# Two attentions on one core: a root taken on VectorE instead of GpSimd, and GpSimd's pieces in another order

## What is computed

```
tgt2 = attention with 16 heads of batch 0 (x[0] asks, ctx[0] answers); x = x + tgt2 for all batches
X = layernorm(ctx) * w1 + b1;  F = layernorm(x) * w2 + b2
attended = softmax(F X^T / 16) X
h = gelu(attended fc1^T + b)                      # 4 features per token
cross = h fc2^T + b2                              # 256 features, but of rank 5
nc = layernorm(cross) * w3 + b3
selfatt = softmax(nc nc^T / 16) nc
out = F + gamma2 * (cross + gamma1 * selfatt)
```

## Time and profile before

| | before |
|---|---|
| median of 3 runs | 236.84 us (236.83 to 241.5) |
| profiled execution | 236.88 us, of which its span 234.8 us |
| TensorE products busy | 209.6 us (89%) |
| VectorE busy | 182.5 us (78%) |
| ScalarE busy | 153.8 us (66%) |
| GpSimd busy | 146.7 us (62%) |

### The profile page before, as it was taken

One profiled execution on the slowest core, in us unless ns is written; L12 is line 12 of the kernel. 1 busy time (PEld: TensorE's weight loads), 2 busy tenths in 40 slices (PEclk: granted clock), 3 DMA queues, 4 the chain that ended last, 5 costly groups with the idle time before them and its releaser, 6 DMA issues.

```text
span 234.8 us, 4965 instructions
## 1 busy us (share of the span) xinstructions
PE 209.6 (89%) x1730; PEld 151.6 (65%) x1730; DVE 182.5 (78%) x360; ACT 153.8 (66%) x295; POOL 146.7 (62%) x240
## 2 busy tenths in 40 slices
PE   8999979987779999999999989997998898899760
PEld 8776646776556978789787867794766444454230
DVE  6499977779979988878778999993333867988673
ACT  2177865544546877778777896789558786677520
POOL 6536551467499999987987793934953288322320
PEclk9999999999999999999999999999999999999855
DMA  6990000084540554426535200000000004444458
GB/s 227 384 332 4 1 1 3 0 223 138 178 179 3 179 179 138 149 78 180 179 108 158 94 3 0 6 0 1 3 0 0 3 15 167 179 181 180 183 212 324
DMA packets 14712, 26.81 MB, mean 114 GB/s; under 512 B 1760, under 2 KB 1760, under 8 KB 14688
## 3 DMA queue, kind: packets, MB, share of 16 engines
q1 hardware_dynamic: 14400, 25.98, 32.3%
q10 hardware_dynamic: 288, 0.52, 0.7%
HBM read 18.11 MB, written 8.39 MB: 113 GB/s over the span
## 4 chain that ended last, share of the span: by engine, by line
PE 53%; DVE 20%; ACT 10%; POOL 8%; issue 6%; DVEq 0%; ACTq 0%; POOLq 0%
PE psum L1085 15%; PE psum L1022 9%; PE psum L1093 5%; DVE xN L381 4%; DVE bn L361 4%; PE psum L970 3%; PE psum L1123 3%; DVE Fall L596 2%; DVE hmax L399 2%; PE psum L1105 2%; PE psum L1205 2%; DVE nmax L523 2%; ACT L862 2%; PE psum L1238 1%; ACT E L887 1%
## 5 line engine op out<-in xcount | busy, mean ns | idle before, releaser
L1085 PE MATMUL psum<-XT,Fall 128*128 128x256 f32 x256 | 61.0, 381 | 1.7 <-ACT Fall L857 1.7
L1085 PEld LDWEIGHTS psum<-XT,Fall 128*128 128x128 f32 x256 | 46.1, 190 | 7.3 <-ACT Fall L857 2.3
L700 POOL TENSOR_SCALAR cN<-cN,nmean,rstd 128x256 f32<-128x256 f32 x64 | 37.4, 594 | 2.5 <-POOL rstd L687 2.1
L680 POOL TENSOR_TENSOR xN<-xN,tgt 128x512 f32<-128x512 f32 x28 | 35.6, 1277 | 4.8 <-DVE xN L381 4.8
L687 POOL TENSOR_TENSOR rstd<-vps,minus_half 128x8 f32<-128x8 f32 (+1 forms) x16 | 24.2, 1512 | 19.9 <-DVE vps L372 19.6
L887 ACT ACTIVATE E<-psum,nmax 128x256 f32<-128x256 f32 x64 | 26.8, 474 | 11.9 <-DVE nmax L523 11.9
L880 ACT ACTIVATE PT<-psum 128x512 f32<-128x512 f32 x32 | 19.1, 598 | 22.7 <-PE psum L1093 22.6
L523 DVE TENSOR_REDUCE nmax<-psum 128x2 f32<-128x512 f32 x32 | 22.0, 687 | 14.7 <-PE psum L1085 14.2
L381 DVE TENSOR_SCALAR xN<-xN,bn,rstd 128x256 f32<-128x256 f32 x64 | 32.8, 558 | 0.5 <-POOL rstd L687 0.4
L581 DVE TENSOR_REDUCE nm<-psum 128x4 bf16<-128x1024 f32 x16 | 19.5, 1220 | 8.2 <-PE psum L1173 8.2
L854 ACT ACTIVATE XT<-psum,b1s,w1s 128x512 f32<-128x512 f32 x32 | 23.0, 795 | 4.0 <-PE psum L1022 4.0
(11 more groups left out here) (173 smaller groups left out, 351.9 us busy)
## 6 DMA issues: line engine op xcount, KB each, us to landing
cN<-ctx SPq DMA_DIRECT2D x32, 256.0 KB, 3.0
xN<-x SPq DMA_DIRECT2D x32, 256.0 KB, 4.1
out<-Fall SPq DMA_DIRECT2D x32, 256.0 KB, 2.3
x0T<-x0t ACTq DMA_DIRECT2D x1, 256.0 KB, 3.0
c0T<-c0t ACTq DMA_DIRECT2D x1, 256.0 KB, 3.9
wqT<-wqt SPq DMA_DIRECT2D x1, 256.0 KB, 3.6
wkT<-wkt SPq DMA_DIRECT2D x1, 256.0 KB, 4.1
wvT<-wvt SPq DMA_DIRECT2D x1, 256.0 KB, 4.8
```

Of the source, the lines that this page charges most:

```text
L680: pool.tensor_tensor(xN[:, b % SLOTS, :], xN[:, b % SLOTS, :], tgt2[:, :, :].rearrange("p t d -> p (t d)"), ALU.add).then_inc(y_ok, 1)
L700: pool.tensor_scalar(own, own, nmean[:, p % 4, NT * m + t:NT * m + t + 1], root_of(p, 0, m, t), ALU.add, ALU.mult)\
L1085: last = pe.matmul(bank[SBANK1[b % 3]][:, t * N:(t + 1) * N], Fall[:, b, c, t * P:(t + 1) * P], XT[:, p % 4, c, m * N:(m + 1) * N], start= ...
```

## The change

For the last eight batches (`quarter(1)`) the root is no longer a power on GpSimd but eleven instructions on VectorE (`second_root`): a shift and a seed on the bits, and three Newton steps of three instructions each. They stand in VectorE's step 5. GpSimd's `scaled` is split into `variances` and `scaled`; `variances(1)` stands right behind `squares(1)`, `scaled(1)` waits for VectorE's count of `alg`, and `right(2)` moves from behind `keyed(1)` to ahead of `output_cuts(1)`. `second_left(1)` on VectorE no longer waits for GpSimd's root.

```diff
@@ second_left(h)
             dve.wait_ge(summed_ok, 8 * (h + 1))
-            dve.wait_ge(rooted_ok, 7 * (h + 1))
+            if h == 0:
+                dve.wait_ge(rooted_ok, 7)
@@ VectorE, new
+        def second_root():
+            G = quarter(1)
+            v, y = var[:, G], r3[:, G]
+            dve.wait_ge(rooted_ok, 12)
+            link(dve.tensor_scalar(y.bitcast(I32), v.bitcast(I32), 1, None, ALU.logical_shift_right))
+            link(dve.tensor_scalar(y.bitcast(I32), y.bitcast(I32), -1.0, RSQRT_SEED, ALU.mult, ALU.add))
+            for _ in range(NEWTON - 1):
+                newton(v, y, t3[:, G])
+            newton(v, y, t3[:, G])
+            ALG["root"] = count[0]
@@ VectorE, steps of the second attention
             if p == 2:
                 second_left(0)
+            if p == 5:
+                second_root()
             if p == 8:
                 second_left(1)
@@ GpSimd
-        def scaled(h):
+        def variances(h):
...
-            rooted(pool.tensor_tensor(y, var[:, G], minus_half[:, 0:GROUP // 2], ALU.pow))
+            if h == 0:
+                rooted(pool.tensor_tensor(y, var[:, G], minus_half[:, 0:PART], ALU.pow))
+
+        def scaled(h):
+            G = quarter(h)
+            y = r3[:, G]
+            if h == 1:
+                pool.wait_ge(alg, ALG["root"])
...
         squares(0)
+        variances(0)
         scaled(0)
         keyed(0)
         right(1)
         squares(1)
+        variances(1)
         output_cuts(0)
         scaled(1)
+        right(2)
         output_cuts(1)
         keyed(1)
-        right(2)
```

## The result

The changed kernel takes 244.83 us (median of 4, 244.69 to 248.07) against 236.84; the ratio is 1.037 (95% interval 1.0265 to 1.0476), so it is slower: by 8.0 us in the medians and by 8.8 us in the ratio, where 5.85 were forecast. By the median it lies within the stated range (240.6 to 245.0), by the ratio (245.6 us) above it. The profiled execution took 244.77 us. The ratios leave out executions that took over 1.5% longer than the fastest of their kernel, all with a lower mean clock; the 248.07 us (mean clock 0.914, the others 0.944 to 0.945) are just under that and count, which is why ratio and medians differ.

The account below looks back on a forecast made before the run. It took the end to hang on GpSimd's order, with TensorE without slack at `output_turn(1)`; 4.44 (stall) + 2.1 (clock) - 0.69 (wait gone) = 5.85 on 236.88 gave 242.7 us, range 240.6 to 245.0.

Parts of the forecast that it names:

- Variances at no cost: GpSimd's five variance instructions, 1.73 us, move into its 5.49 us of idle time before `output_cuts(0)`, and cost nothing.
- The root's start and price: VectorE's step 5, behind `finish(0)`: starts at 192.47, eleven links of 0.22 us, 2.42 us in all, ends at 194.89.
- The stall: TensorE at `output_turn(1)`: starts at 199.18 instead of 194.74, 4.44 us later, by VectorE's late root and `right(2)`.
- Covered delay of VectorE: `maxima(7)` and `finish(1)` behind the root end at 197.15, before 199.18, so the stall covers the delay.
- What comes back: TensorE's wait for GpSimd at `output_turn(2)` goes: 0.69 us back, at most 0.5 with TensorE at full speed.
- rival with a held clock: Clock stays up through TensorE's idle time at `output_turn(1)`: 4.44 - 0.5 = 3.9, 240.8 us; chance 0.25, hardly falling included.
- The clock: TensorE's 5.1 us idle before `output_turn(1)` brings the granted clock down to half speed, costing 2.1 us.
- the time at half speed: Behind the stall: 5.9 us of work at half speed, as at the kernel's start, losing 2.1 us.
- half speed lasts longer: Rival: low level behind the stall lasts 10 us, 244.4 us; to the end, about 253; chance 0.14.
- The end: Behind step 10 nothing is changed and TensorE sets the pace, so the rest shifts as a whole.

Follow-up runs that it names:

- one half each: Two kernels: the changed one with `right(2)` back behind `keyed(1)`, no ratio (240.04, 243.79 to 244.29 us); the one before with `right(2)` ahead of `output_cuts(1)`, 1.0203.
- 19 fillers: Changed kernel with 19 filler products on TensorE in step 6, ahead of its wait for `output_cuts(1)`: ratio 1.0129; runs of 239.89, 239.92, 246.54 and 247.14 us.

## Why the prediction was right and wrong

The direction, the place and the mechanism of the stall were right; the size of one term was not. Step by step:

- *Variances at no cost.* Right: `output_cuts(0)` ends at 186.70, and with the 1.19 us of the earlier start that is 187.89; before, GpSimd went on to the next piece at 187.83.
- *The root's start and price.* Right. It starts where `maxima(7)` stood; eleven links took 2.29 us (191.28 to 193.57), 0.21 each where 0.22 was taken. The estimate of 1.9 us from the Trainium skill's formula ("VectorE: DVE Perf Modes", section "The TRN2 errata — SBUF-src ops pay a fixed extra latency per instruction") is lower, as said. The trace agrees with its 0.174 us for one instruction: the two-input ones took 0.17 to 0.18 us. The handover comes on top.
- *The stall.* Right: 4.21 us for a forecast of 4.44; the 0.13 of the links and the rest of handovers make the difference. The experiments with one half each, 2.24 and 2.01, show its two parts as the sum had them.
- *Covered delay of VectorE.* Right: `maxima(7)` and `finish(1)` are through by 195.9, before the stall ends.
- *What comes back.* As forecast in the changed kernel, where `output_turn(2)` waits for nobody; wrong at full speed. The rival with a held clock gave 0.5 back at `maxima_turn(10)`; with 19 fillers `maxima_turn(10)` comes 9.88 us behind `output_turn(1)`, as before (9.89). I had let it wait for `maxima(10)`, but for even steps it also waits for the `co` of `returned(3)`, which stands behind `maxima(10)` and `second_left(1)` on VectorE. The row says so (0.94 for VectorE's L602).
- *The clock.* That it falls was right. **The step that failed is the time at half speed:** I took 5.9 us from the kernel's start and priced them at 2.1 us; behind the stall's end it lasted 18.3 us. The 5.95 us that this cost are net of the 0.69 that came back, so that 6.6 us stand against the 2.1. The price per us was right: 6.6/18.3 = 0.36, as 2.1/5.9. What was wrong is to carry the length over from the start. What sets the length stays open. With 12 of the start's filler products the clock was back in some 4 us behind the stall, in both profiles; with the steps' own products the stretch was anything from 6.8 to 20.5 us long. The rival "half speed lasts longer", with 10 us and 244.4, came nearest, in the time by luck: its 10 us are about half of what was measured, and the start and the end hid 2.1 us. Its ground against it ("busy for 1.00 of 1.00 us, as at the start") was the same mistake.
- *The end.* Not in the sum: before, the clock fell at 221 to 222 and the last products ran at half speed; in the changed kernel they ran at full speed, and 0.9 us came back. The 19-filler kernel shows the same. The change does not touch this place. Eight of the twelve other profiles show the same 0.8 to 0.9 us against the kernel before and four do not, and the runs do not settle why; in the comparison it is luck, as is the start.

So the sum of 4.44 + 2.1 - 0.69 = 5.85 should have read 4.21 + 5.95 - 0.9 = 9.3, of which this execution's faster start hid 1.2. With the start of before this execution would have taken about 246.0 us (244.77 + 1.19, an estimate), above the range.

## What to carry to other kernels

Work that is moved to another engine comes when that engine's queue reaches it: before counting what the first engine saves, find the time at which the other can begin, and what stands behind the wait. The same change cost 8 us with its eleven instructions in step 5 and gained 1 with them in step 3; leaving the power where it was and moving it into a gap of its own engine gained as much without any of them. A stall of TensorE has two prices, its length and the stretch at half speed behind it, and here the second was the larger. A gap that can't be closed may be worth filling: with 19 fillers two of four runs took 239.9 us, but the other two 246.5 and 247.1, more than without.

## What was not expected of the hardware

After the stall the granted clock stayed at 0.50 for 18 us (two profiles: 18.3 and 18.4) while TensorE went on with the steps' own products; with 4.97 us of 128x128 fillers first it was back at 1.00 after 4.3 and 3.9. The busy time of the profile, 2.00 of 2.00 us, does not tell the two apart. Nor does the length of a wait tell whether the clock falls and for how long: waits of 0.81 and 0.89 us were followed by 6.8 us at 0.50, one of 2.69 by 10.2, one of 2.91 by 17.1, while the kernel before went through this wait of 1.22 us with the clock at 1.00 behind it:

```profile
164.00 0.44 PE L1113 MATMUL psum<-ident,vT 128*128 128x128 f32 x2 [1.22 <-ACT vT L868]
```

And the start of the kernel, which the change does not touch, moved everything behind it by up to 1.6 us between the profiles (`maxima_turn(5)` at 187.80 to 189.38): by the end of the stretch at half speed (the first eight products take 2.71 us or 1.97), or by the arrival of `wkT` (0.71 us of waiting). A difference of that size between two profiles is no effect of a change until that place has been looked at.
